# First stage of a four-stage transformer kernel: attention numerator and denominator from one product with tokens on partitions, residuals added on VectorE, all ReLU on ScalarE

## The reference, cut to what matters

```
h  = layernorm(x)                                   # no scale, no shift
Q, K, V = h Wq+bq, h Wk+bk, h Wv+bv                 # 16 heads of 8
Q, K = elu(Q)+1, elu(K)+1
KV, Ksum = K^T V per head and sequence, sum of K over the sequence
num = Q KV;  den = Q Ksum + 1e-6;  att = num / den
r1 = h + att Wo + bo;   y = layernorm(r1) g1 + beta1
r2 = y + relu(y W1 + b1) W2 + b2
x  = x + layernorm(r2) g2 + beta2
```

## Time and profile before

| | |
|---|---|
| runs of the kernel | 845.48, 846.76, 848.72 us |
| the profiled execution | 845.9 us, of it 844.0 us span |
| busy over the span | PE 81%, DVE 65%, POOL 56%, ACT 40% |
| stage A, from the start to the next stage's first statistics | 176.3 us |
| pitch of a full body of stage A | 8.6 to 8.7 us |

### The profile page before, as it was taken

The page is one execution under the profiler, slowest core; times in us unless marked ns, Lnnn a source line. Parts: engine busy times, 40 slices in busy tenths (PEclk is TensorE's granted clock), DMA queues, the critical chain, the costliest instruction groups (busy, mean ns, idle before and its releaser), DMA issues.

```text
span 844.0 us, 18577 instructions
## 1 busy us (share of the span) xinstructions
PE 687.7 (81%) x5238; PEld 579.5 (69%) x5238; DVE 547.8 (65%) x1972; ACT 338.1 (40%) x839; POOL 476.0 (56%) x1098
## 2 busy tenths in 40 slices
PE   5799999877888754999969999995788876089994
PEld 3588888734666653999955877774566755079994
DVE  3788887556999854688842333323489985248885
ACT  2332323125777510555532121220677762045552
POOL 5465656643688870388764233322348887127886
PEclk9999999979999857899988999998799995579997
DMA  7900000040011134233230000004001111423320
GB/s 225 291 13 15 12 19 13 26 106 2 13 39 37 45 126 87 73 86 93 72 108 18 20 13 19 19 14 118 1 2 38 46 42 45 82 73 87 93 84 31
DMA packets 54887, 49.50 MB, mean 59 GB/s; under 512 B 5768, under 2 KB 49743, under 8 KB 54704
## 3 DMA queue, kind: packets, MB, share of 16 engines
q1 hardware_dynamic: 46426, 33.51, 14.8%
q0 software_dynamic: 5568, 13.54, 4.5%
q10 hardware_dynamic: 2838, 1.78, 1.1%
HBM read 31.07 MB, written 19.85 MB: 60 GB/s over the span
## 4 chain that ended last, share of the span: by engine, by line
PE 45%; DVE 23%; POOL 9%; issue 8%; DMA 6%; ACT 4%; DVEq 1%; SPq 1%; ACTq 1%; POOLq 1%
PE bank L1260 7%; PE wide L1397 7%; PE bank L1386 7%; PE wide L1271 4%; DVE early L1029 4%; DVE early L736 3%; POOL rstd L534 3%; DVE stats L511 2%; PE bank L1271 2%; PE wide L456 2%; DVE z L538 2%; DMA sorted_dram<-sorted_dram 2%; POOL sorted_dram L1114 1%; PE wide L871 1%; DMA sorted_dram<-rows_e,pos 1%
## 5 line engine op out<-in xcount | busy, mean ns | idle before, releaser
L520 POOL TENSOR_TENSOR both_m<-stats 128x2 f32<-128x2 f32 (+1 forms) x94 | 19.1, 203 | 175.1 <-DVE stats L511 174.7
L1219 POOL TENSOR_TENSOR rstd<-var_e,half_neg 128x1 f32<-128x1 f32 x78 | 59.0, 756 | 84.3 <-DVE var_e L1322 79.4
L1260 PE MATMUL bank<-zt,late 128*128 128x128 f32 x624 | 90.9, 291 | 1.6 <-issue 1.2
L534 POOL TENSOR_TENSOR rstd<-spread_m,half_neg 128x2 f32<-128x2 f32 (+1 forms) x94 | 86.0, 915 | 7.4
L1260 PEld LDWEIGHTS bank<-zt,late 128*128 128x128 f32 x624 | 78.8, 198 | 8.3 <-issue 4.0
L1114 POOL DMA_INDIRECT sorted_dram<-rows_e,pos x64 | 66.7, 1043 | 15.5 <-issue 14.7
L1312 DVE TENSOR_SCALAR hid_f<-bank 128x256 f32<-128x256 f32 x78 | 33.1, 425 | 49.6 <-PE bank L1260 44.9
L1386 PE MATMUL bank<-late,qk_t 128*128 128x128 f32 x512 | 62.1, 275 | 0.0
L1293 ACT ACTIVATE late<-we 128x512 f32 x78 | 49.2, 631 | 28.6 <-PE bank L1260 24.4
L1397 PE MATMUL wide<-vo,gram 128*128 128x512 f32 x128 | 60.0, 612 | 0.7 <-ACT gram L1444 0.7
L1386 PEld LDWEIGHTS bank<-late,qk_t 128*128 128x128 f32 x512 | 59.6, 192 | 0.0
(11 more groups left out here) (247 smaller groups left out, 1878.9 us busy)
## 6 DMA issues: line engine op xcount, KB each, us to landing
rows_e<-sorted_dram SPq DMA_DIRECT2D x78, 128.5 KB
xa<-x_dram SPq DMA_DIRECT2D x9, 640.0 KB, 6.4
we<-L_ffn_W SPq DMA_DIRECT2D x16, 256.0 KB
x_dram<-xout SPq DMA_DIRECT2D x32, 128.0 KB, 1.8
rows_e<-L_ffn_b SPq DMA_DIRECT2D x1, 2048.0 KB
xa<-L_attn_a_x SPq DMA_DIRECT2D x3, 512.0 KB, 6.1
sorted_dram<-sorted_dram ACTq DMA_DIRECT2D x8, 128.5 KB, 6.4
sorted_dram<-sorted_dram SPq DMA_DIRECT2D x8, 128.5 KB, 6.8
```

Source lines behind the costliest of these rows:

```text
L534: nc.gpsimd.tensor_tensor(rstd[:, slot, w], spread_m[:, slot, 0, w], half_neg[:, w], ALU.pow).then_inc(rstd_made, 1)
L1219: nc.gpsimd.tensor_tensor(rstd[:, s % 3, 0:1], var_e[:, s % 3, :], half_neg[:, 0:1], ALU.pow).then_inc(g["rstd"], 1)
L1260: last = nc.tensor.matmul(to[:, (m % 2) * P:(m % 2 + 1) * P], we_t[:, c1, m * P:(m + 1) * P], zt[:, c1, 0, 0:P], start=True, stop=True)
```

## The change

In step 2 the two masked matrices become one of 128x144: 128 columns of numerator and 16 of key sums, one for each head. q_t is now the stationary operand, so that one product for each tile of 128 tokens gives numerator and denominator with tokens on partitions (bank ND, 144 columns a tile). DVE adds 1e-6 to the 128x32 denominators, takes their reciprocal, and multiplies with it repeated over eight columns into att_r. Since Wo needs features on partitions, PE then transposes att_r into a free half of bank 6 (AT), and ACT copies it to att_t.

The products with ra0 and ra1 go. POOL makes xz = z0 + bo and y1 = z1 * g1 (each 128x256); DVE adds xz to the Wo product (r1), y1 to the W2 product, and then c1 = beta1 + b2 to that (r2), and takes statistics and normalises from SBUF. The mean and variance of r1 now come from DVE's bn_aggr, and POOL does two instructions in place of eight for it. Both halves of ReLU are ACT's. The denominator's copy on ACT goes. The orders within the bodies change, the loop is unrolled by 4 in place of 2, x is loaded in 4 parts (2, 8, 10 and 12 tiles) in place of 5, and loads_a has 14 DMAs in another order, of which six repeat a row over 128 partitions, in place of 12 with two such. The later stages are changed in semaphore counts only.

```diff
-                    nc.tensor.matmul(ND[:, 0:256], kv[:, c, 0, :], q_t[:, c, :], start=True, stop=True)
-                    nc.tensor.matmul(ND[:, 256:512], kv[:, c, 1, :], q_t[:, c, :], start=True,
-                                     stop=True).then_inc(g["att"], 1)
+                    for t in range(2):
+                        last = nc.tensor.matmul(ND[:, t * NDW:(t + 1) * NDW], q_t[:, c, t * P:(t + 1) * P], kv[:, c, 0:NDW],
+                                                start=True, stop=True)
...
-                        last = nc.tensor.matmul(WO[:, cut], zt[:, l, 0, cut], ra0[:, :], start=False, stop=True)
...
-                        last = nc.tensor.matmul(to[:, cut], zt[:, c, 1, cut], ra1[:, :], start=False, stop=True)
...
+                    nc.vector.tensor_tensor(y1[:, (s - 6) % 4, :, :], w2[:, 0:256].rearrange("p (t d) -> p t d", t=2),
+                                            y1[:, (s - 6) % 4, :, :], ALU.add).then_inc(g["r2"], 1)
...
+                    nc.vector.tensor_tensor(r2[:, c, :, :], y1[:, (s - 6) % 4, :, :],
+                                            c1_a[:, :].unsqueeze(1).to_broadcast([P, 2, D]), ALU.add).then_inc(g["r2"], 1)
...
+                    dve.wait_ge(g["wo"], i - 2)
+                    dve.wait_ge(g["xz"], i - 2)
+                    nc.vector.tensor_tensor(r1[:, l, :, :], WO.rearrange("p (t d) -> p t d", t=2), xz[:, (s - 3) % 4, :, :],
+                                            ALU.add).then_inc(g["r1"], 1)
...
-                    nc.vector.tensor_scalar_max(hid[:, l, 2:4, :], WH[:, 512:1024].rearrange("p (m t) -> p m t", m=2),
-                                                0.0).then_inc(g["relu_b"], 1)
...
-                    nc.vector.reciprocal(den[:, c, :], den[:, c, :]).then_inc(g["inv"], 1)
-                    dve.wait_ge(g["inv"], i - 1)
-                    nc.vector.tensor_tensor(att_t[:, c, :], ND[:, 0:256], den[:, c, :], ALU.mult).then_inc(g["att_t"], 1)
+                    nc.vector.reciprocal(rden[:, c, :], rden[:, c, :]).then_inc(g["inv"], 1)
+                    dve.wait_ge(g["inv"], i * 2 - 2)
+                    for t in range(2):
+                        last = nc.vector.tensor_tensor(
+                            att_r[:, c, t, :].rearrange("p (h d) -> p h d", h=HA),
+                            ND[:, t * NDW:t * NDW + P].rearrange("p (h d) -> p h d", h=HA),
+                            rden[:, c, t * HA:(t + 1) * HA].unsqueeze(2).to_broadcast([P, HA, P // HA]), ALU.mult)
...
+                    nc.gpsimd.tensor_tensor(xz[:, s % 4, :, :], z0[:, c, :, :], bo_a[:, :].unsqueeze(1).to_broadcast([P, 2, D]),
+                                            ALU.add).then_inc(g["xz"], 1)
...
+                    nc.gpsimd.tensor_tensor(y1[:, (s - 3) % 4, :, :], z1[:, l, :, :],
+                                            g1_a[:, :].unsqueeze(1).to_broadcast([P, 2, D]), ALU.mult).then_inc(g["y1"], 1)
```

More of the change, by code:

```diff
@@ L221, in build @@
         row_f, row_a, row_a2 = row_f[0:1], row_a[0:1], row_a2[0:1]
-        k_r, exp_q, exp_k, kv, den, xres = parts(
-            early[:, 0:HALF], (2, 2, P), (2, 2 * P), (2, 2, P), (2, 2, P), (2, 2 * P), (2, 2, D))
+        k_r, exp_q, exp_k, kv, att_r, xres = parts(
+            early[:, 0:HALF], (2, 2, P), (2, 2 * P), (2, 2, P), (2, 2 * P), (2, 2, P), (2, 2, D))
         hid, = parts(hid_f, (2, FC, 2 * P))
@@ L545, in build @@
         a_s = {n: sem("a_" + n) for n in (
[L546 to L548 removed]
+            "stats0", "stats1", "stats2", "step", "step1", "rstd", "rstd1", "z0", "z1", "turned", "turned1", "zt", "zt1",
+            "kv_q", "exp_q", "v", "phi", "sums", "masked", "att", "inv", "att_r", "att_turned", "att_t",
+            "wo", "xz", "r1", "hid", "relu", "w2", "y1", "r2", "xres", "tmp", "x1", "var1")}
+        c1_made = sem("c1_made")
         a_stored = [sem(f"a_stored{n}") for n in range(2)]
[L550 to L551 removed]
+        A_DEPTH, A_FIRST, A_UNROLL = 7, 8, 4
+        TT, QM, KV, ND, WO, W2B = bank[0], bank[1], bank[2], bank[3], bank[6][:, 0:256], bank[7]
+        AT = bank[6][:, 256:512]
         WH = wide[:, 0:1024]
+        NDW = P + HA
         W2_TURNS = PAIRS - 3
@@ L693, in body @@
+                if has(2):
+                    dve.wait_ge(g["sums"], i - 1)
+                    nc.vector.tensor_tensor(kv[:, c, 0:P], QM[:, 256:256 + P], blk8[:, :], ALU.mult)
+                    nc.vector.tensor_scalar(kv[:, c, P:NDW], blk8[:, :].rearrange("p (h d) -> p h d", h=HA)[:, :, 0],
+                                            QM[:, 256 + P:256 + P + 1], None, ALU.mult).then_inc(g["masked"], 1)
                 if has(3):
                     dve.wait_ge(g["wo"], i - 2)
-                    bn([WO[:, 0:P], WO[:, P:2 * P]], c, 4, g["stats1"])
@@ L705, in body @@
+                if has(3):
+                    for t in range(2):
+                        last = nc.vector.bn_aggr(mv_a[:, l, t, :], stats[:, c, 4 + t, :])
+                    last.then_inc(g["step1"], 1)
                 if has(0) or has(6):
                     dve.wait_ge(g["rstd"], i + 1)
-                if has(6):
-                    for t in range(2):
-                        last = nc.vector.scalar_tensor_tensor(out=tmp[:, c, t, :], in0=w2[:, t * P:(t + 1) * P],
-                                                              scalar=mean[:, c, 0, 2 + t:3 + t], in1=g2a[:, :],
-                                                              op0=ALU.add, op1=ALU.mult)
-                    last.then_inc(g["tmp"], 1)
@@ L717, in body @@
                 if has(6):
+                    for t in range(2):
+                        last = nc.vector.scalar_tensor_tensor(out=tmp[:, c, t, :], in0=r2[:, c, t, :],
+                                                              scalar=mean[:, c, 0, 2 + t:3 + t], in1=g2a[:, :],
+                                                              op0=ALU.add, op1=ALU.mult)
+                    last.then_inc(g["tmp"], 1)
+                if has(1):
+                    dve.wait_ge(g["exp_q"], i)
+                    nc.vector.scalar_tensor_tensor(out=q_t[:, l, :], in0=exp_q[:, l, :], scalar=1.0,
+                                                   in1=QM[:, 0:256], op0=ALU.min, op1=ALU.max).then_inc(g["phi"], 1)
+                if has(2):
+                    dve.wait_ge(g["att"], i - 1)
+                    pieces = ND[:, 0:2 * NDW].rearrange("p (t n) -> p t n", t=2)
+                    nc.vector.tensor_scalar_add(rden[:, c, :].rearrange("p (t h) -> p t h", t=2), pieces[:, :, P:],
+                                                1e-6).then_inc(g["inv"], 1)
+                if has(6):
                     dve.wait_ge(g["tmp"], i - 5)
                     dve.wait_ge(g["xres"], i - 5)
-                    after(dve, a_stored[c], lap(8) * 16 + 16)
+                    after(dve, a_stored[c], lap(8, 2) * 16 + 16)
                     for t in range(2):
@@ L746, in _ @@
             dve.wait_ge(stats_init, 1)
[L747 removed]
+            pipeline(dve, PAIRS, A_DEPTH, A_UNROLL, body, A_FIRST)
         @on("gpsimd")
@@ L812, in build @@
         sorted_ = [sem(f"m_sorted{k}") for k in range(3)]
-        x_back = [sem(f"m_x{k}") for k in range(len(G_PARTS))]
+        assert len(G_PARTS) == len(X_PARTS)
         wb_in = sem("wb_in")
```

205 lines of the change are left out of this document (110 added, 95 removed).

## The result

The changed kernel takes 850.57 us in the median of 20 runs, the kernel before 847.12 on the same chip. The ratio is 1.0039, with a 95% interval of 1.0028 to 1.005: slower by 0.4%, where the forecast was 0.6% faster. It lies inside "within 0.5%", but the sign is wrong. 850.57 is 0.07 above the upper end of the range, 850.5; put on the forecast's base (846.76 times 1.0039, thus 850.1) it is just inside.

A forecast was written before the change was run, and what follows sets the result against it. Stage A's PE - DVE - PE loop was taken to bound the kernel, POOL's root 0.3 us behind. Gains 1.9 + 3.0 + 0.2 = 5.1 us took 845.9 to 840.8; the median's 0.9 made 841.7 us, range 835.5 to 850.5.

The forecast's parts named there:

- within 0.5%: Outcome class for no change, about 4.2 us either way; given 0.34, against 0.45 for faster and 0.21 for slower.
- Locks: Slower rival, chance 0.21: POOL's xz and xres hold DVE's xout, 0.72 us in each of ten full bodies, total 848.9 us.
- r1's wait: In each full body DVE stands still 1.46 us from the mask's end until PE's Wo product arrives.
- The walk: One pass round a full body's PE and DVE loop: 1.46 + 4.80 + 2.07 = 8.33 us, against 8.66 before.
- Root rival: Faster rival, chance 0.15: Wo is ready early, POOL's root bounds the full body at 7.8 us, total 836.4 us.
- Full bodies: Stage A's ten full bodies gain 0.33 us each, 3.3 us, taken as 3.0.
- the 0.3 taken off for z1: Full bodies' gain cut from 3.3 to 3.0 us, since z1 has only 0.2 us between it and POOL's xres.
- Bodies 0 to 5: Stage A's start: body 1 starts at 15.3, body 6 at 46.0 against 47.94; gain 1.9 us.
- Start rival: No-change rival, chance 0.20: slow broadcast loads cost 1 us, body 1's unhidden hat and waits 2 to 3; total 845.5 us.
- The hat in body 1: PE's 512-column hidden-layer hat moves into body 1; forecast hidden, since PE waits there anyhow.
- The hold of z1 in body 5: Before the full bodies, 0.15 to 0.7 us a body allowed where z1 meets POOL's xz or xres.
- The drain: Stage A's last bodies: 16 to 18 gain 1.1, 0.5, 0.3, the last three lose 0.3, 0.9, 0.9; gain about 0.2 us.

The follow-up runs named there:

- x_late: Changed kernel with DVE's two xout instructions moved behind the reciprocal and att_r; ratio 0.9974 to the kernel before, full-body pitch 8.35 us.
- no_xres: Changed kernel without POOL's addition of beta2 (xres), DVE's xout reading xa directly; ratio 0.9971 to the kernel before, pitch 8.42 us.
- before_lock: Kernel before, with POOL's addition of beta2 moved ahead of its second root, waiting for z0, to lie beside DVE's xout; ratio 1.0035.
- before_lock_b: Kernel before, with POOL's addition of beta2 ahead of its second root, waiting for tmp, to lie beside DVE's xout; ratio 1.0118, pitch 9.08 us.
- wo_first: Changed kernel with PE's Wo product issued ahead of the wait for the mask and of Q; ratio 0.9961 to the kernel before, pitch 8.36 us.
- loads: Changed kernel with the six broadcast rows issued last on ACT's queue, with their own semaphore; ratio 1.0058 to the kernel before.
- rows_late: Changed kernel with the six broadcast rows on SP's queue behind x's second part, and POOL's first xz in body 1; ratio 1.0069 to the kernel before.

## Why the prediction was wrong

**The step that failed** is "by that rule xout and tmp, which now both read two SBUF tensors, are held too; I count no hold for them". xout is held by POOL's 128x256 instructions in every full body, for 0.68 us (1.29 against 0.61), 6.8 us in ten bodies. x_late, no_xres and both before_lock kernels show it from four sides; no_xres and before_lock_b also tell it from a slowness of the operands themselves. The rival Locks had the place (6.4 to 6.9 of the body beside xz and xres) and the price (0.72 us), and its total of 848.9 us stands 1.7 under the median measured. That this is so near is in part luck: the full bodies without the hold, the start and the drain were each off too, as told below. The ground given against it was that L722 ran beside POOL's small instructions at its usual time, and that no row had it beside a 128x256 one. The second is no evidence, and the nearest row of a 128x256 one, a tensor_scalar's, said held. The Trainium skill's rule ("GPSIMD Engine Reference", section "8. Key points") agrees with the runs for two SBUF inputs (xout 1.28 us for 0.61), and the prediction cited it and set it aside.

**One premise behind that step was off too**: xout read tmp and xres, both in SBUF, before the change. What changed is not its operands but its neighbours: POOL got xz and now does xres at the time of xout.

**The loop.** r1's wait of 1.46 us was forecast to the hundredth, and its parts agree with the rows too (Q 0.06 behind the mask, the transposes 0.53 behind Q, Wo 0.22 behind them). The reciprocal at 0.35 came at 0.34. The walk's 8.33 us is 0.11 over the 8.22 that the changed kernel's pitch less the hold gives; x_late's 8.35 belongs to another order of the blocks, so that match is luck. The Root rival fell for the reason given: PE does wait for "masked". wo_first shows what it left out, that Wo need not wait with Q.

**Full bodies**: forecast -3.0, measured +2.5 us; +6.8 are locks, so the rest is -4.3: 3.3 from the walk and 1.1 since it was 0.11 too long for each body; the 0.3 taken off for z1 did not come.

**Bodies 0 to 5**: forecast -1.9, measured +0.2. The Start rival's sign came beside that of Locks: body 6 starts after 47.5, and body 1 at 16.75 (forecast 15.3) is outside the 14 to 16 given. At body 1 the four more broadcast rows and two more DMAs cost more than their landing rate; how the 1.45 us divide isn't shown, but loads shows that x also waits while such rows are in flight. The hat in body 1, on which that rival laid 2 to 3 us, cost nothing that shows: bodies 1 and 2 took 10.0 us, 10.3 forecast. Bodies 3 and 4 took 14.6, 13.3 forecast, and there x_late, the same program up to body 6, took 12.9: the difference is the half-clock stretch at 33.7 us, 1.7 us in this execution, which the prediction had at nothing, since the kernel before has none between 18 and 45 us. The hold of z1 in body 5 (1.03 us) was allowed for, and body 5 took the 7.1 forecast. rows_late shows that body 1 does not decide body 6: 5.1 us sooner there are 0.4 at body 6.

**The drain**: forecast -0.2, measured +2.8 us. The starts of tmp divide it; in the changed kernel the last three are

```profile
163.72 1.07 DVE L746 SCALAR_TENSOR_TENSOR tmp<-late,mean,g2a 128x128 f32<-128x128 f32 x2 [2.73 <-POOL rstd L537]
...
169.78 1.07 DVE L746 SCALAR_TENSOR_TENSOR tmp<-late,mean,g2a 128x128 f32<-128x128 f32 x2 [2.72 <-POOL rstd L537]
...
175.53 0.61 DVE L746 SCALAR_TENSOR_TENSOR tmp<-late,mean,g2a 128x128 f32<-128x128 f32 x2 [2.72 <-POOL rstd L537]
```

The distances of the last three bodies are 6.59, 6.06 and 5.75 us, before 6.29, 5.17 and 4.38: 2.6 lost, where 2.1 was forecast. In the three bodies ahead 0.7 is gained, where 1.9 was forecast; in each of them xout is held again (1.08 to 1.10 us for 0.61), and r2's second addition is held by y1 at 145.78, 153.16 and 159.76 (0.72 for 0.44). The way from the last tmp to stage F is 0.7 shorter (6.22 against 6.92; 0.35 forecast). And 1.9 us were not counted at all: in a full body tmp follows the x statistics after 5.1 us, before after 3.2, and the drain pays this once. The sum against body 15 is 3.1, and 2.8 from body 16 on, since a pitch is 0.25 longer. Inside the last three the W1 product runs at a granted clock of 0.5 (3.47 us, 1.99 in the kernel before), and tmp is held twice by xres (1.07 for 0.61):

```profile
160.36 3.47 PE L631 MATMUL wide<-zt,wa 128*128 128x256 f32 x8 [0.47 <-ACT zt L672]
```

Of the clock 0.3 us is on the path: in x_late the same tmp follows the one ahead after 5.76 us with W1 at full clock, here after 6.06. How much of each hold is on the path was not tried apart.

**The chances.** 0.21 for Locks was too low where the rule that the prediction cites and the nearest row both spoke for it. It was also put in the wrong class: Locks' own total, 848.9 us, is 0.25% over 846.76, thus "within 0.5%" and not "slower". By the rivals' own totals the class that came had 0.55 and not 0.34.

## What to carry to other kernels

Before giving GpSimd a wide instruction, write down what VectorE does at that moment: here scalar_tensor_tensor and tensor_tensor with two SBUF inputs and tensor_scalar with one were held until GpSimd's was done, and those that read PSUM weren't. Order both queues so that these don't meet, and check the held instruction's neighbours, since a swap hands the hold to the next. And in a loop over two engines, look on the engine that waits for work in its queue that doesn't need the wait: the moves of Wo and q_t, on top of x_late, took the ratio from 0.9974 to 0.9849, 1.25%, where the change itself was forecast to give 0.6%. And before pricing a half-clock stretch between two profiles, compare the stage up to the edit: it can be there in one execution of the same instructions and not in another.
